# A state-space block behind a resampled pointwise block: the input product in two instructions, a 98x97 grid, no filler matmuls, the residual by transposes

## Time and profile before

| what | value |
|---|---|
| median of 3 runs | 6347.22 us |
| span of the profiled execution | 6343.7 us; its own time is not listed beside it, the median of the runs lies 3.5 us above the span |
| TensorE (PE) busy | 6036.5 us, 95% |
| VectorE (DVE) busy | 5685.5 us, 90% |
| ScalarE (ACT) busy | 5097.3 us, 80% |
| GpSimd (POOL) busy | 5209.8 us, 82% |
| DMA | 983 MB, 65% of 16 engines |
| mean granted TensorE clock | 0.965 of full |

### The profile page before, as it was taken

One profiled execution on the slowest core, in us unless ns is written; L12 is line 12 of the kernel. 1 busy time (PEld: TensorE's weight loads), 2 busy tenths in 40 slices (PEclk: granted clock), 3 DMA queues, 4 the chain that ended last, 5 costly groups with the idle time before them and its releaser, 6 DMA issues. The chain is left out here.

```text
span 6343.7 us, 99100 instructions
## 1 busy us (share of the span) xinstructions
PE 6036.5 (95%) x32260; PEld 3123.0 (49%) x32260; DVE 5685.5 (90%) x4459; ACT 5097.3 (80%) x8658; POOL 5209.8 (82%) x5092
## 2 busy tenths in 40 slices
PE   8999999999999999999999999999999999998776
PEld 5645445454554545545455544545455454554222
DVE  0089999999999999999999999999999999999998
ACT  4588888888888888888888788888888888887664
POOL 0078888888888888888888888888888888888988
PEclk9999999999999999999999999999999999998665
DMA  3367676676767667675676767667676766767553
GB/s 95 88 165 170 160 167 157 163 162 169 169 154 168 155 165 170 155 182 142 167 162 162 173 156 169 155 164 163 167 169 156 166 154 165 168 142 160 129 124 75
DMA packets 805826, 983.25 MB, mean 155 GB/s; under 512 B 391258, under 2 KB 417542, under 8 KB 805318
## 3 DMA queue, kind: packets, MB, share of 16 engines
q1 hardware_dynamic: 805318, 976.92, 65.4%
HBM read 717.71 MB, written 259.00 MB: 154 GB/s over the span
## 5 line engine op out<-in xcount | busy, mean ns | idle before, releaser
L1181 POOL TENSOR_TENSOR hc<-hs,cs 128x512 f32<-128x512 f32 x3072 | 3835.6, 1271 | 692.7 <-DVE hs L1140 505.6
L1140 DVE TENSOR_TENSOR_SCAN hs<-av,state,b 128x512 f32<-128x512 f32 x2688 | 3257.8, 1263 | 88.6 <-POOL state L1185 4.9
L1008 ACT ACTIVATE av<-rep_d,nega 128x512 f32<-128x512 f32 x3072 | 2096.7, 713 | 41.5 <-DVE hs L1140 36.8
L1134 DVE TENSOR_TENSOR b<-rep_u,pb 128x1536 f32<-128x1536 f32 x1024 | 1803.5, 1761 | 211.0 <-PE pb L846 124.7
L855 PE MATMUL py<-hc,rsel 128*32 128x512 f32 x6144 | 1141.6, 634 | 40.6 <-POOL hc L1181 39.7
L769 PE MATMUL cb<-xu,w1a 96*128 96x392 f32 x2400 | 984.3, 513 | 27.7 <-DVE b1a L1120 17.4
L774 PEld LDWEIGHTS cb<-w2c,g 128*98 128x98 f32 x9600 | 885.9, 167 | 169.7 <-issue 106.9
L774 PE MATMUL cb<-w2c,g 128*98 128x96 f32 x9600 | 910.7, 252 | 17.4 <-ACT g L956 9.3
L956 ACT ACTIVATE g<-cb,b1a 128x392 f32<-128x392 f32 x1200 | 679.5, 579 | 87.0 <-PE cb L769 78.8
L810 PE MATMUL cb<-xn,wtap 96*96 96x512 f32 x1536 | 723.3, 607 | 2.4 <-ACT xn L1029 2.4
L769 PEld LDWEIGHTS cb<-xu,w1a 96*128 96x128 f32 x2400 | 414.5, 191 | 415.4 <-issue 199.3
(11 more groups left out here) (109 smaller groups left out, 6703.4 us busy)
## 6 DMA issues: line engine op xcount, KB each, us to landing
rep_d<-delta_scratch SPq DMA_DIRECT2D x512, 384.0 KB, 7.0
rep_u<-deltax_scratch SPq DMA_DIRECT2D x512, 384.0 KB, 6.3
cs<-c_scratch SPq DMA_DIRECT2D x512, 256.0 KB, 5.9
delta_scratch<-dlt SPq DMA_DIRECT2D x128, 384.0 KB, 3.1
deltax_scratch<-dlt SPq DMA_DIRECT2D x128, 384.0 KB, 9.2
t1r<-t_scratch SPq DMA_DIRECT2D x160, 240.0 KB, 6.5
v_scratch<-v2s SPq DMA_DIRECT2D x192, 192.0 KB
xb<-in_x SPq DMA_DIRECT2D x128, 192.0 KB, 4.6
```

Of the source, the lines that this page charges most:

```text
L1008: act.activation(av[:, n % NAV, :], rep_d[:, k % 2, j, :], ACT.Exp, scale=nega[:, q, j:j + 1])\
L1134: dve.tensor_tensor(b3[:, :, :], rep_u[:, k % 2, 3 * hf:3 * hf + 3, :], pb[:, None, :].broadcast_to([128, 3, T]), ALU.mult).then_inc(dve_b ...
L1140: dve.tensor_tensor_scan(hs[:, n % NHS, :], av[:, n % NAV, :], b3[:, n % 3, :], start, ALU.mult, ALU.add)\
L1181: pool.tensor_tensor(hc[:, n % NHC, :], hs[:, n % NHS, :], cs[:, k % 2, g % NQ, :], ALU.mult)\
```

## The change

1. The product of u and B of a group is two instructions: units 0 and 1 in one, unit 2 in the other. The first waits only for the second-last scan of the group before, the second for the last. The first scan waits for the first product (`dve_b2`), the third scan for the second (`dve_bu`).
2. The plans have no WARM steps.
3. The fine grid has 98 x 97 points in place of 100 x 98. There are still 25 blocks; the last one has 2 columns in place of 4.
4. The residual in `OUT` enters by `pe.transpose` ahead of the two matmuls, in place of a matmul with the identity behind them. The planner's cost of OUT is 2.25 us in place of 2.70.

```diff
-GW, GH = 100, 98
-NB = GW // 4
+GW, GH = 98, 97
+NB = (GW + 3) // 4
...
+def wide(b):
+
+    return min(4, GW - 4 * b)
...
-         "X": 2.72, "Z": 0.92, "DBC": 1.82, "DT": 0.50, "OUT": 2.70, "WARM": 0.215}
+         "X": 2.72, "Z": 0.92, "DBC": 1.82, "DT": 0.50, "OUT": 2.25, "WARM": 0.215}
...
-    return padded(rows + (warm(rows) if kind != "tail" else []))
+    return padded(rows)
...
-                src = t1_d[bass.ds(w, 1)].rearrange("o w f -> (o w f)").rearrange(
-                    "(i p c) -> p i c", p=128, c=C)[:, 5 * m:5 * m + 5, :]
-                sp.dma_start(t1r[:, m % 2], src).then_inc(t1_ld[m % 2], 16)
+                    "(i p c) -> p i c", p=128, c=C)[:, 5 * m:5 * m + n, :]
+                sp.dma_start(t1r[:, m % 2, 0:n], src).then_inc(t1_ld[m % 2], 16)
...
-                    for e in range(2):
+                    for e in range(wide(b) // 2):
...
-                    mm = pe.matmul(bank[:, 0:BC], w1a[:, 128 * f:128 * f + 128], xu[:, b % 2, :],
+                    n = wide(b) * GH
+                    mm = pe.matmul(bank[:, 0:n], w1a[:, 128 * f:128 * f + 128], xu[:, b % 2, 0:n],
...
-                    for j in range(4):
+                    for j in range(wide(b)):
...
+                    pe.transpose(o, x1o[:, tb], ident[0:C, 0:C])
                     for t in range(2):
-                        pe.matmul(o, xcs[:, p, t, tb], wo[:, t, :], start=(t == 0), stop=False)
-                    mm = pe.matmul(o, x1o[:, tb], ident[0:C, 0:C], start=False, stop=True)
+                        mm = pe.matmul(o, xcs[:, p, t, tb], wo[:, t, :], start=False, stop=(t == 1), skip_group_check=True)
...
                 if n % 3 == 0:
 
                     dve.wait_ge(pe_b, count(pe_b, G * NG + g + 1))
+                    dve.wait_ge(dve_h, count(dve_h, G * NU + n - 1))
+                    dve.tensor_tensor(b3[:, 0:2, :], rep_u[:, k % 2, 3 * hf:3 * hf + 2, :],
+                                      pb[:, None, :].broadcast_to([128, 2, T]), ALU.mult).then_inc(dve_b2, 1)
                     dve.wait_ge(dve_h, count(dve_h, G * NU + n))
-                    dve.tensor_tensor(b3[:, :, :], rep_u[:, k % 2, 3 * hf:3 * hf + 3, :],
-                                      pb[:, None, :].broadcast_to([128, 3, T]), ALU.mult).then_inc(dve_bu, 1)
+                    dve.tensor_tensor(b3[:, 2, :], rep_u[:, k % 2, 3 * hf + 2, :], pb[:, :], ALU.mult).then_inc(dve_bu, 1)
                     dve.wait_ge(pool_st, count(pool_st, G * NG + g + 1 - NHS // 3))
+                    dve.wait_ge(dve_b2, count(dve_b2, G * NG + g + 1))
+                if n % 3 == 2:
                     dve.wait_ge(dve_bu, count(dve_bu, G * NG + g + 1))
```

More of the change, by code:

```diff
@@ L346, in build @@
         act_a = sem("act_a")
+        dve_b2 = sem("dve_b2")
         dve_bu = sem("dve_bu")
@@ L510, in load_t1 @@
             def load_t1(w, m):
+                n = min(5, GW // 2 - 5 * m)
                 src = t1_d[bass.ds(w, 1)].rearrange("o w f -> (o w f)").rearrange(
-                    "(i p c) -> p i c", p=128, c=C)[:, 5 * m:5 * m + 5, :]
-                sp.dma_start(t1r[:, m % 2], src).then_inc(t1_ld[m % 2], 16)
+                    "(i p c) -> p i c", p=128, c=C)[:, 5 * m:5 * m + n, :]
+                sp.dma_start(t1r[:, m % 2, 0:n], src).then_inc(t1_ld[m % 2], 16)
             def load_rr(d, m):
@@ L573, in step @@
                     sp.sem_inc(sp_passed, 1)
-                    rows = HH * min(2, NB - 2 * b)
-                    dst = v2_d[x, :, 8 * b:8 * b + rows // 16, :].rearrange("h (e w) c -> e h (w c)", w=4)
-                    sp.dma_start(dst, v2s[0:rows, b % 2]).then_inc(v2_st[b % 2], 16)
+                    two, w = min(2, NB - 2 * b), wide(2 * b)
+                    dst = v2_d[x, :, 8 * b:8 * b + two * w, :].rearrange("h (e w) c -> e h (w c)", w=w)
+                    sp.dma_start(dst, v2s[0:HH * two, b % 2, 0:w * C]).then_inc(v2_st[b % 2], 16)
                 if name == "ST":
@@ L779, in step @@
                         half = slice(HH * (e % 2), HH * (e % 2) + HH)
-                        mm = pe.matmul(bank[half, 0:4 * C], dn_h[:, :], vr[:, e % 2, :], start=True, stop=True)
+                        n = wide(e) * C
+                        mm = pe.matmul(bank[half, 0:n], dn_h[:, :], vr[:, e % 2, 0:n], start=True, stop=True)
                 elif name == "DG":
@@ L935, in step @@
                 elif name == "W_up":
-                    out, src = xu[:, b % 2, :], bank[0:C, 0:BC]
+                    n = wide(b) * GH
+                    out, src = xu[:, b % 2, 0:n], bank[0:C, 0:n]
                 elif name == "W_2":
-                    out, src = vr[:, b % 2, :], bank[0:GH, 0:4 * C]
+                    n = wide(b) * C
+                    out, src = vr[:, b % 2, 0:n], bank[0:GH, 0:n]
                 elif name == "W_dn":
                     act.wait_ge(v2_st[b % 2], count(v2_st[b % 2], x * (16 * (7 - b % 2)) + (b // 2) * 16))
-                    rows = HH * min(2, NB - 2 * b)
-                    out, src = v2s[0:rows, b % 2, :], bank[0:rows, 0:4 * C]
+                    rows, n = HH * min(2, NB - 2 * b), wide(2 * b) * C
+                    out, src = v2s[0:rows, b % 2, 0:n], bank[0:rows, 0:n]
                 elif name == "ST":
@@ L955, in step @@
                         act.wait_ge(cb_free[w % RING], st.freed(w))
-                    act.activation(g2[:, b % 2, f, :], bank[:, 0:BC], ACT.Square, bias=b1a[:, f:f + 1]).then_inc(fr, 1)
+                    n = wide(b) * GH
+                    act.activation(g2[:, b % 2, f, 0:n], bank[:, 0:n], ACT.Square, bias=b1a[:, f:f + 1]).then_inc(fr, 1)
                 elif name in ("D_lo", "D_hi"):
```

## The result

The kernel takes 6306.8 us after the change (median of 4 runs, 6304.1 to 6309.2) against 6346.3 before (4 runs): a ratio of 0.9941, with a 95% interval of 0.9927 to 0.9955. It is faster, but by 39.5 us and not by the 165 forecast, and the time lies above the forecast range (6070 to 6280). The span of the profiled execution goes from 6343.7 to 6307.0.

The account below looks back on a forecast made before the run. VectorE and TensorE were taken as both full, within 2% of each other. Savings of 8.8 us a sample over 14 samples (123), tail 19, last 19 and start-up 4 made 165, giving 6182 us; range 6070 to 6280.

Parts of the forecast that it names:

- The change, OUT: Output step on TensorE: a transpose replaces two matmul instructions, saving 0.44 us an OUT, 3.1 a sample in heavy stretches.
- the sum: Whole kernel: 8.8 us a sample over 14 samples, tail 19, last 19, start-up 4; together 165, giving 6182.
- (c): TensorE stays at 1.2 GHz from group 29 far into the heavy stretch: 84 us slower, 6430; chance 0.06.
- Relief of TensorE and VectorE together: Heavy stretches, 342.1 us a sample: TensorE work falls by 7.9, VectorE's floor would allow 26; 10 taken.
- The clock without WARM: Light stretch and the heavy one behind: TensorE falls to 1.2 GHz, charged 3 us a sample, bounds 0 and 8.
- The grid and OUT: TensorE work saved a sample: 3.9 us by the smaller grid, 3.1 by the transposes in OUT.
- The tail: Tail sample: TensorE busy 311 of 364, so VectorE sets it; 64 groups at 0.30 save 19 us.
- rival (b): GpSimd becomes the bound, VectorE averages no lower than 5.45 a group: 76 us saved, 6271; chance 0.15.
- The group's floor: VectorE's time for a group with the split product: 5.28 us where it took 5.58, bounds 5.20 and 5.78.
- VectorE's waits for `pb`: Waits for the spread of B, forecast to grow from 7.5 to some 20 us a sample.
- Groups 34 to 47 longer than the 85.6 of before: Heavy stretch behind the light one: taking more than 85.6 us was named as a sign of a wrong prediction.
- rival (d): Nothing overlaps in the split product: 5.78 us a group, 96 us slower, 6443; chance 0.04.

## Why the prediction was wrong, step by step

**The step that failed.** "The change, OUT" counts the instructions of OUT and nothing else. It passes over the line of the diff that sets OUT's cost in the plan to 2.25, and the sum takes the heavy stretches' order of work as that of before. By the ratios this line is worth 98 us in the changed kernel (0.9941 against 0.9786) and 105 in the kernel before (1.0165). Moving two steps back recovers 96 of the 98 (0.9789); `W_f` alone recovers 62 (0.9843) and `W_2` alone 23 (0.9904), so the two together cost somewhat more than each by itself. The mechanism is shown end to end: the step moves, OUT waits 2.13 for a bank held behind ScalarE's softplus, the clock falls, groups 7 and 8 take 5 us more. The diff alone held it: a planner's cost is an input of the order. None of the rivals named it. (c) had the clock, but at another place and from another cause.

**The sum otherwise.** With the old order the kernel takes 6203 where 6182 was forecast, inside the range. By the traces of that run and of before, an undisturbed sample gives about 7 us and not 8.8 (25 over 14 samples), the tail 13.5 and not 19, start-up 7 and not 4; the last sample 19 as forecast. Four of its terms:

- *Relief of TensorE and VectorE together.* I took 10 us for the heavy stretches. They went from 342.1 (undisturbed, before) to 337.1 in sample 9 of that run, so 5.0, while TensorE's busy time in them fell by 7.1 (337.7 to 330.6), near the 7.9 forecast. The relief of TensorE was sized about right; what it pays was put above it and lies below it. The split alone gives 68 us, of it hardly 1 a sample in the heavy stretches: "two engines within 2% of each other" was the right reading of the earlier trace rows. Together the parts are worth more than singly: split 68, transposes 17 and grid 33, less 10 for WARM (medians), are 108, and all of them in the old order give 138.
- *The clock without WARM*, charged 3 a sample: 0.7 in the kernel before, 0.3 in the changed one, nothing with the old order. The spreads in the light stretch do take 0.61 and 0.63, and 0.38 again at 3920.25, so the clock falls where the earlier trace rows said it would. With the old order groups 34 to 47 take 85.0 in ten of samples 1 to 13, and in all of them with WARM, so the cushion of the earlier trace rows swallows it there but for three samples. With the moved `W_2` it does not: 88.4 in the mean without WARM, 86.7 with it.
- *The grid and OUT*, 3.9 and 3.1 a sample: alone they give 33 us, 6 of them in the start-up, and 17 us; that is 2.3 a sample (mean of samples 1 to 13) and 1.2. TensorE's work in a group is not all on the path.
- *The tail*, 19, with VectorE taken to set it alone: 13. Its waits for `pb` grow from 2.6 us in all to 9.2 in the changed kernel. The largest place is group 18, where a reduce waits 3.68 for GpSimd's `hc` (L1197) and TensorE then runs at 1.2 GHz; the group takes 9.0, and 5.6 before. That is the lumpy work of GpSimd that rival (b) had in mind, at a smaller size.

The light stretch with its slow spreads in sample 9 of the changed kernel (TensorE):

```profile
3898.61 0.61 PE L855 MATMUL pb<-bc,selb 96*128 96x512 bf16 x1 [1.75 <-DVE b L1149]
...
3914.91 0.63 PE L855 MATMUL pb<-bc,selb 96*128 96x512 bf16 x1
...
3920.25 0.38 PE L855 MATMUL pb<-bc,selb 96*128 96x512 bf16 x1
```

**What was right.** The group's floor: 1.13 and 0.58 of the queue forecast, 1.11 and 0.60 measured; 5.25 to 5.28 forecast, 5.24 measured; last sample's window 333 forecast, 332.6 measured; light stretch 31.7 and 31.5; a block of OUT 0.56 and 0.53 (4002.34 to 4002.87). VectorE's waits for `pb` grew to what was forecast, some 20 a sample, but in part by luck, since 7 of them are the two stalls: 22.3 in sample 9 of the changed kernel, 15.2 with the old order (to be read beside the earlier trace rows):

```profile
DVE b L1146 <- PE pb L855: 22.3, 27, 3.7
```

```profile
DVE b L1146 <- PE pb L855: 15.2, 26, 1.8
```

"Groups 34 to 47 longer than the 85.6 of before" was named as the sign of a wrong prediction, and it was one: 87.1, by the second wait.

VectorE: DVE Perf Modes in the Trainium skill (Terms) has the next operation wait until the pipe is empty, by which rival (d) gave 6443. The second product starts at 6209.15 and the first ends by its record at 6209.25; the last sample measured 332.6 where 63 groups of 5.78 are some 364. No run here agrees with it. TensorE: Matmul & The Clock Gate in the Trainium skill (Part 4) says that transposes don't count as busy in the same way; the transposes alone gave 0.9974 and the fall of the clock behind OUT's wait is there with matmuls in their place, so no run here shows that it mattered.

## What to carry to other kernels

A number that a planner reads is part of the schedule: when a diff changes one, lay the old and the new order side by side and price every step that moves, and what each in-order queue has ahead of it in its buffer ring. Where two engines are both full, a busy time taken off either is worth only a part of itself (here 2.5 of 19 us a sample for the split, 1.2 of 3.1 for the transposes, 2.3 of 3.9 for the grid). A buffer that comes late from an engine busy with table loads can cost twice: here the wait of 2.13 us, and the slow clock that followed it in all of samples 1 to 13; the wait of 1.37 was followed by it in six.

## What the runs showed of the chip

- One matmul step of 0.9 us, put ahead of OUT in TensorE's queue, cost 62 us in 6300 (4.4 us a sample): 2.1 of wait, and most of the rest is work at 1.2 GHz in two groups.
- After the wait of 2.13 us between full stretches the clock is at 1.2 GHz for the spread of group 8 and at 2.4 GHz again for that of group 9, in all of samples 1 to 13 of the changed kernel.
- 48 unread matmuls a sample, 44 of them (10.4 us of TensorE's busy time) in the light stretch, were worth 0.14% in the kernel before and nothing that shows in the changed kernel with the old order (0.9786 without, 0.9784 with).
- Less work made it slower: without OUT's residual transposes the kernel took 27 us more. At group 24 the 0.36 us taken off became a longer wait for ScalarE, and the clock fell there in six of samples 1 to 13, where it fell in none with the transposes.
- Two steps put back give 0.9789 and the whole old order 0.9786, within their intervals, so the other seven moves cost nothing that shows.
